# Projections and denominators behind the weighted sums of their period in a fused attention and quantised feed-forward kernel

## What is computed

```python
x = x + attn(layernorm(x), w_qkv, w_out, b_out)
x = x + ffn(layernorm(x), w_gate, w_up, w_down)
# attn: q, k, v = split(x @ w_qkv); softmax(q k^T / 8) v, heads joined, @ w_out + b_out
# ffn:  silu(q4(x) @ q4(w_gate).T) * (q4(x) @ q4(w_up).T) = h;  q4(h) @ q4(w_down).T
# q4: per block of 16, scale = max|x|/6, each value to the nearest of 0, .5, 1, 1.5, 2, 3, 4, 6 (signed)
```

## Time and profile before

| | |
|---|---|
| median of three runs | 1360.01 us |
| the profiled execution | 1359.78 us, span 1357.6 us |
| PE busy | 1273.8 us, 94% |
| POOL busy | 1054.4 us, 78% |
| ACT busy | 904.2 us, 67% |
| DVE busy | 807.9 us, 60% |
| mean granted clock of PE | 0.98 |
| chain that ended last | PE 84%, DVE 7%, issue 5%, POOL 2%, ACT 1% |

### The profile page before, as it was taken

The page is one execution under the profiler, slowest core; times in us unless marked ns, Lnnn a source line. Parts: engine busy times, 40 slices in busy tenths (PEclk is TensorE's granted clock), DMA queues, the critical chain, the costliest instruction groups (busy, mean ns, idle before and its releaser), DMA issues.

```text
span 1357.6 us, 24832 instructions
## 1 busy us (share of the span) xinstructions
PE 1273.8 (94%) x7541; PEld 675.7 (50%) x7541; DVE 807.9 (60%) x2238; ACT 904.2 (67%) x1300; POOL 1054.4 (78%) x457
## 2 busy tenths in 40 slices
PE   4999999999999999999999999999999998898566
PEld 3555555555455555555455555555555554443245
DVE  6655555556555555565555555555555557786694
ACT  4777677777677677767677677767776777554243
POOL 4488888898788888889788888888898888779132
PEclk9999999999999999999999999999999999899687
DMA  2000000000000000000000000000000000000001
GB/s 63 2 9 2 1 2 9 1 1 2 3 10 1 2 1 9 1 1 1 5 8 1 2 2 9 1 2 1 4 1 2 1 2 1 1 1 0 1 1 31
DMA packets 45950, 6.65 MB, mean 5 GB/s; under 512 B 37344, under 2 KB 45664, under 8 KB 45808
## 3 DMA queue, kind: packets, MB, share of 16 engines
q1 hardware_dynamic: 45584, 4.41, 2.6%
q0 software_dynamic: 224, 0.54, 0.1%
HBM read 3.75 MB, written 1.05 MB: 4 GB/s over the span
## 4 chain that ended last, share of the span: by engine, by line
PE 84%; DVE 7%; issue 5%; POOL 2%; ACT 1%; DMA 0%; POOLq 0%; SPq 0%; DVEq 0%; ACTq 0%
PE o_ps L1157 32%; PE s_ps L1005 24%; PE mx_ps L1027 8%; PE mx_ps L1020 4%; PE misc_ps L1147 3%; PE misc_ps L1139 2%; PE misc_ps L976 2%; PE misc_ps L988 1%; PE s_ps L1013 1%; PE misc_ps L977 1%; PE misc_ps L978 1%; POOL acc_pool L499 1%; PE misc_ps L989 1%; PE misc_ps L990 1%; PE s_ps L1247 1%
## 5 line engine op out<-in xcount | busy, mean ns | idle before, releaser
L499 POOL TENSOR_TENSOR acc_pool<-acc_pool,probs 128x1024 f32<-128x1024 f32 x352 | 853.4, 2424 | 49.4 <-POOL acc_pool L499 41.6
L792 DVE CUSTOM_DVE_ANT_0 summed<-mx_ps,rise 128x512 bf16<-128x512 f32 x503 | 344.9, 686 | 382.5 <-issue 338.0
L616 ACT ACTIVATE probs<-s_ps 128x1024 f32<-128x1024 f32 x512 | 525.6, 1027 | 70.1 <-PE s_ps L1005 30.0
L1157 PE MATMUL o_ps<-probs,vv 128*64 128x512 f32 x2048 | 497.1, 605 | 7.6 <-ACT probs L616 7.6
L536 ACT ACTIVATE rise<-mx_ps 128x512 f32<-128x512 f32 x503 | 299.8, 596 | 278.6 <-PE mx_ps L1020 267.8
L1157 PEld LDWEIGHTS o_ps<-probs,vv 128*64 128x64 f32 x2048 | 126.8, 136 | 232.1 <-issue 180.6
L1027 PE MATMUL mx_ps<-k_hi,q_hi 64*128 64x512 f32 x503 | 223.8, 445 | 8.8 <-issue 5.1
L1020 PE MATMUL mx_ps<-k_raw,q_hi 64*128 64x512 f32 x503 | 223.9, 445 | 8.4 <-DVE part_max L792 7.2
L1005 PE MATMUL s_ps<-q_hi,k_hi 64*128 64x512 f32 x1024 | 204.7, 394 | 0.9 <-ACT probs L616 0.8
L1005 PE MATMUL s_ps<-q_hi,k_lo 64*128 64x512 f32 x1024 | 203.0, 391 | 0.0
L1005 PE MATMUL s_ps<-q_lo,k_hi 64*128 64x512 f32 x1024 | 202.0, 389 | 0.0
(11 more groups left out here) (161 smaller groups left out, 1123.1 us busy)
## 6 DMA issues: line engine op xcount, KB each, us to landing
mrow<-neg_max SPq DMA_DIRECT2D x256, 0.5 KB, 2.0
wqkv<-in_L_attn_w_qkv SPq DMA_DIRECT2D x8, 192.0 KB, 3.1
y<-in_L_attn_x SPq DMA_DIRECT2D x4, 256.0 KB, 4.4
out<-y SPq DMA_DIRECT2D x4, 256.0 KB, 2.3
wo<-in_L_attn_w_out SPq DMA_DIRECT2D x8, 64.0 KB, 1.9
wx<-in_L_ffn_w_down POOLq DMA_DIRECT2D x1, 176.0 KB, 6.3
wx<-in_L_ffn_w_gate POOLq DMA_DIRECT2D x1, 128.0 KB, 4.6
wx<-in_L_ffn_w_up POOLq DMA_DIRECT2D x1, 128.0 KB, 4.9
```

The lines of the kernel that those rows point to most:

```text
L499: pool.tensor_tensor(acc, first, probs[:, j % P_BUFS, :, :], ALU.add) \
L616: act.activation(probs[:, j % P_BUFS, :, :], s_ps[:, j % 2, :, :], ACT.Exp, scale=SCALE) \
L792: dve.tensor_tensor_reduce(summed[:, s % 2, :], mx_bank(h, pair), rise[:, h, :], 1.0, LOWEST, ALU.add, ALU.max, part_max[:, slot:slot + 1] ...
L1157: ins = pe.matmul(o_ps[DH * h:DH * (h + 1), :], vv[par(w)][:, j, DH * h:DH * (h + 1)], probs[:, j % P_BUFS, h, :], start=(j == 0), stop=(j ...
```

## The change

PE issues the misc work of a period after its two weighted sums, not before them. VectorE empties what PE now makes later one tile later: the low parts of K and Q at j = 2 and 10 where it was 1 and 9, the reciprocals at j = 6, 7, 7 and 8 where it was 5, 5, 6 and 7, the normalisation at j = 9 where it was 8, the addition of the projection at j = 12 where it was 11. ACT's, POOL's and SyncE's programs are the same.

```diff
-INVERT_AT = {DEN_AT: (0, 1), DEN_AT + 1: (2,), DEN_AT + 2: (3,)}
+INVERT_AT = {DEN_AT + 1: (0,), DEN_AT + 2: (1, 2), DEN_AT + 3: (3,)}
...
-                        if j == K_AT and not skipped("K", w, last):
+                        if j == K_AT + 1 and not skipped("K", w, last):
                             dve.wait_ge(hi_done, kq_no(it, w, "K", last))
                             k_low(1 - par(w), w % CHUNKS, misc_ps[:, :]).then_inc(misc_free, 1)
                         for t in INVERT_AT.get(j, ()):
                             invert(it, w, last, t)
-                        if j == DEN_AT + 3:
+                        if j == DEN_AT + 4:
                             normalise(it, w, last)
-                        if j == Q_AT and not skipped("Q", w, last):
+                        if j == Q_AT + 1 and not skipped("Q", w, last):
                             dve.wait_ge(hi_done, kq_no(it, w, "Q", last))
                             q_low((w + 2) % Q_BUFS, misc_ps[:, :]).then_inc(misc_free, 1)
-                        if j == PROJ_AT:
+                        if j == PROJ_AT + 1:
                             add_projection(it, w, last)
...
                         if j % 2:
                             row_maxima(it, w, last, j)
+                        if j % 2:
+
+                            weighted(it, w, j - 1)
+                            weighted(it, w, j)
                         if j in misc_at(w, last):
                             misc(misc_at(w, last)[j], it, w, last)
-                        if j % 2:
-
-                            weighted(it, w, j - 1)
-                            weighted(it, w, j)
```

More of the change, by code:

```diff
@@ L1200, in body @@
                             row_maxima(it, w, last, j)
-                        if j in misc_at(w, last):
-                            misc(misc_at(w, last)[j], it, w, last)
                         if j % 2:
@@ L1206, in body @@
                             weighted(it, w, j)
+                        if j in misc_at(w, last):
+                            misc(misc_at(w, last)[j], it, w, last)
             with pe.Fori(0, ITERS - 1) as it:
```

## The result

The changed kernel takes 1371.26 us (median of four runs, 1370.09 to 1373.80) where the kernel before takes 1360.64 us (median of four, 1358.38 to 1362.92): a ratio of 1.0076, 95% interval 1.0057 to 1.0095. It is slower by 10.6 us, where 4.1 were forecast, and lies above the range. The profiled execution took 1373.8 us, span 1371.9.

A forecast was written before the change was run, and what follows sets the result against it. TensorE was taken to bound the loop, busy 298.4 of 301.0 us a turn. The profiled 1359.8 us + 1.9 (tile 9) + 1.2 (normalisation) + 1.0 (last turn) gave 1363.9, forecast as a median of 1364.1 us, range 1358 to 1369.

The forecast's parts named there:

- PE's own work: PE's matmuls in the new order: crossings between kinds of work cost the same, 0 us, bounds -27 to +13 us.
- The cheaper crossing: Rival at the start of misc after the sums: 0.09 to 0.19 us saved per crossing, 13 to 27 us; chance 0.08.
- the low bound: Crossings from sums to misc: the load of misc's first weights hides under the last weighted sum, -27 us.
- SyncE's load of the output weights waits for the projection and goes 1.9 us later, with a unit to spare: SyncE's output-weight load, listed among what hides: later by 1.9 us but covered, costed at nothing.
- The wait at tile 9: Two reciprocals in tile 7 delay tile 8's maximum; PE loses 0.08 us in 24 units, +1.9 us, bounds 0 to 7.
- The normalisation in w = 2 and 6: VectorE, tile 9: normalisation waits for POOL's addition; PE loses 0.2 us in 6 units, +1.2 us, bounds 0 to 5.
- ACT's evictions behind a cover of 0.1 us: K and Q evictions start about 1.9 us later, still in time, costed at nothing; 5 us if the cover fails.
- The last turn: Units 5 to 7: VectorE's small steps and projection addition shift onto the chain, +1 us, from -2 to +5 us.
- the forecast's gain: Last turn, unit 5: PE's idle time is split, the clock may stay at 2.4 GHz, up to 1.8 us come back.
- What would show it: The prediction's list of expected trace signs: loop turn 302.0 us, short wait at tile 9, unit times telling the cases apart.
- thin covers: Rival: normalisation late in all units, K/Q rise late, or a missed gap in the last turn; about 1368 us; chance 0.12.

The follow-up runs named there:

- run 8: Run 7 with SyncE's load of output weights also moved behind the row-maximum DMAs: 1361.56 us, ratio 0.9997 to the kernel before.
- run 3: Kernel before with the load of output weights split into four DMAs of 32 rows, lengthening SyncE's queue: 1366.20 us, ratio 1.0038.
- run 1: Changed kernel with SyncE's wait for the projection and load of output weights moved behind the row-maximum DMAs: 1366.35 us, ratio 1.0037.
- run 7: Changed kernel with denominators back in front of the sums, reciprocals and normalisation at their old tiles, SyncE's queue as changed: 1367.54 us, ratio 1.0044.
- run 6: Run 1 with reciprocals regrouped, one at tile 6, one at tile 7, two at tile 8: 1363.18 us, ratio 1.0015 to the kernel before.
- run 5: Kernel before with only PE's new order, misc behind the weighted sums, VectorE's list unchanged: 1430.59 us, ratio 1.0511.
- run 2: Kernel before with SyncE's load of output weights moved behind the row-maximum DMAs: 1361.54 us, ratio 1.0012.

## Why the prediction was wrong

**PE's own work: right.** Zero was forecast between -27 and +13 us. The crossing from sums to misc costs what the others cost (1.87 and 0.33 us above), and run 8 measures the order by itself at -0.3 us in the loop. The cheaper crossing did not come: the first load of the K weights starts with its matmul and not under the last sum. The rule of the Trainium skill that was cited for the low bound ("TensorE: Matmul & The Clock Gate", "Step-by-step: what each phase is for", loads pulled ahead) brings nothing at this crossing in this trace; with 128 rows on both sides its condition on row groups is not met, and the trace shows nothing of its other one, the background buffer.

**"SyncE's load of the output weights waits for the projection and goes 1.9 us later, with a unit to spare": the step that failed.** It is true of the load and asks the wrong question. The load has a unit to spare; the 8 DMAs behind it in the same queue had 0.4 to 1.5 us (the estimate at run 3), and the projection moved by 1.9. I followed the moved event to the instruction that waits for it, and not to what is queued behind that instruction. Cost taken: 0. Measured: 6.1 us (result, run 1), made at will by a longer queue (run 3), and separable from all else (run 7 against 8: 6.0 us in the medians).

**The wait at tile 9: right in mechanism, half its size.** 0.08 us a unit was forecast, +1.9 us; it measured 0.16 us, 3.9 us. The pair of reciprocals took 1.76 us (1.77 forecast), the sums stand 0.43 us behind the step (0.43 forecast), and run 6 shows that without the pair the loss goes. What was off is the instant of the step: 0.04 us late instead of 0.03 us early. The forecast left the read of tile 7's maximum where it was (627.23), and it came 0.09 us later, behind the register instruction at tile 6. In the written-out turn, whose waits need no register instructions, the place with the pair loses 0.02 us. With so thin a cover, a tenth of a microsecond in the sum is the whole term. The interval behind was taken right, the lateness had the wrong sign.

**The normalisation in w = 2 and 6: right place, smaller.** 0.11 us in six units, 0.7 us, where 1.2 was forecast. It took 2.17 us where 2.1 was forecast, its mean rose from 1482 to 2034 ns:

```profile
L817 DVE TENSOR_TENSOR o_norm<-o_raw,rden 128x512 f32<-128x512 f32 x33 | 67.1, 2034 | 0.1
```

**ACT's evictions behind a cover of 0.1 us: right.** The K and Q periods lose nothing of their own in the changed kernel or in runs 1, 6, 7 and 8.

**The last turn: +1 us forecast, not to be told from zero.** The idle time of PE in unit 5 was split as the forecast's gain had it, with 2.41 us as the longest wait where it was 4.42, and the unit is 0.6 us shorter; but from its start to the end of the span the changed kernel takes 0.7 us more (223.05 against 222.35 us), and run 1, where PE's and VectorE's lists in that turn are the same, took 224.5. Runs 7 and 8, which are alike from there on, took 221.2 and 224.5. This scatter is larger than the term.

**The sum.** 3.9 + 0.7 + 6.1 = 10.7 us against 10.6 in the medians. Of the 6.5 us that the forecast's 4.1 lacked, 6.1 are the queue and 2.0 tile 9; the normalisation was 0.5 us too high, and the last turn by up to 1. "What would show it" had put 37.5 us and more down to thin covers of VectorE: the loop has units of 37.46 us and, where `maximum(0)` waits, of 37.96 to 38.89, and the waits view, read for `mrow`, tells them apart.

## What to carry to other kernels

When an event moves, follow it to the instruction that waits for it and then down that engine's queue to the next consumer on the critical path; a wait in an in-order DMA queue delays everything behind it, however patient its own transfer is. Where one buffer is handed to and fro, both sides have to move together: each half of this change alone cost 43 and 70 us, both together 10.6. And read intervals between starts, since waits of 0.1 us in each of 24 units are in no list of idle times.

## What the runs showed of the hardware that was not expected

- A wait that PE meets at a row-maximum step costs about 0.11 us on top of the lateness, in the interval behind it, independent of its length (0.04, 0.48 and 0.92 us late, 0.10 to 0.12 each time; in w = 2 and 6 of the change, 0.11 behind a step of tile 11 that is late by 0.01). PE's wait for the `mrow` DMA leaves the same behind it: from `maximum(0)` to the step of tile 15 it is 0.33 or 0.34 us in all 24 such waits (the changed kernel and runs 3, 5 and 7), and 0.23 without a wait. It lies in the same interval as the wait, so the 6.1 us hold six times 0.11.
- The eight row DMAs of a unit do not always take the same time. Behind the load of output weights their starts are mostly 0.5 to 0.75 us apart, but in most such units of the changed kernel one gap is 1.3 to 1.5 us, so the queue takes 5.3 to 5.9 us there, and `maximum(0)` starts 1.45 to 1.85 us behind its end. With both, the waits of one kernel differ from unit to unit.
- The boundary between two turns of the loop is not one number. PE stands idle there for some 2 us in every run (the waits "<- issue" above, 4.5 us in 2 times), and then sometimes runs at a lower clock. Stretches of the changed kernel (columns as in the earlier trace rows), and below them the same place in the kernel before:

```profile
352.00:354.00 2.00, 1.81 (x9) 1.70 (x11) 0.75 (x3) 1.89 (x3) 0.60 (x1) 0.57 0.07 20
354.00:356.00 2.00, 2.00 (x12) 1.54 (x8) 0.00 (x0) 1.02 (x1) 0.12 (x1) 0.58 0.00 0
```

```profile
349.00:354.00 5.00, 4.94 (x29) 2.80 (x29) 1.90 (x7) 3.68 (x6) 2.31 (x2) 1.00 0.02 5
```

  A granted clock of 0.57 is near the lower level, 1.2 GHz. The three intervals around a boundary took 9.78 and 9.89 us before, 10.90 and 11.35 in the changed kernel; but 10.86 and 9.95 in run 2, 10.83 and 11.33 in run 3, 9.30 and 11.30 in run 6, 9.52 and 9.31 in run 8. Of the twenty boundaries in the ten traces, the nine at the lower clock took 10.8 to 11.4 us, the other eleven 9.3 to 10.0. It comes with either order, so it is scatter between executions, up to 2 us a boundary. The changed kernel's profiled execution, the slowest of its four, has 2.6 us of it.
